# A vision tower layer on one core: tile loads three steps later in the sync engine's order, stores two steps later

## The chip, the cores and the metric

The kernel runs on one core of one Trainium2 chip. The metric is device time in microseconds (us) of one execution. Before the change three runs gave 1940.26, 1950.12 and 1956.40 us; their median is 1950.12 us.

## What is computed

The input x is 128 images of 12 channels by 224 by 224 in f32. The layer has three parts:

```python
pooled = x.reshape(Bb, Cc, n, K, n, K).sum(axis=(3, 5))          # 14 x 14 patches of 16 x 16
h = einsum('bcij,ce->bije', pooled, channel_weights)             # 196 tokens of 192 numbers
h = h + attn(layernorm(h))      # the first 64 tokens ask, the other 132 answer; projection of the result
h = h + ffn(layernorm(h))       # 8 routed experts of width 128, the best two of each token; one shared expert
```

The ffn computes `silu(x w1) * (x w3)` for each expert, multiplies it with the token's weight for this expert (zero for six of the eight), multiplies by `w2` and adds over the experts. The shared expert has no weight.

## The kernel before

**Groups, chunks, steps.** The images are worked in 8 groups of 16. The tokens of a group are split into 7 chunks: two of 512 query tokens, then key tokens in chunks of 512, 64, 512, 512 and 512. For each chunk all 9 experts are run one after the other, so a group has 63 steps (STEPS), step = 9 * chunk + expert. All engines follow this count. Every engine has its own program, in the same order of steps, and semaphores tie them together.

**One step.** TensorE (PE) makes h1 and h3 of this expert (L1275 for query chunks, with five products each, L1446 for key chunks), and between them the second layer of the step two before (L1426). ScalarE (ACT) takes silu of h1 (L803). GpSimd (POOL) multiplies it by the row of router weights of this expert, spread over 128 partitions (L654, in `scale`). VectorE (DVE) multiplies that by h3 (L1189) and counts `h_done`. PE may begin step s only when `h_done` of step s-2 is there. The shared expert (the ninth step of each chunk) needs no router weights.

**Router rows.** The weights of a group are computed one group ahead and written to a small array in HBM, `cw_rows`, in steps 57 to 59 (`cw_rows_out`, L496). `cw_load` (L520) reads one row of 512 weights back, spread over all partitions (256 KB written), into one of CW_RING = 7 buffers. The load for step s+5 (CW_AHEAD) stands at step s of the sync engine's order. It waits until the buffer is free, which is `h_done` of the use seven before.

**Tiles.** The images of a group come in 21 tiles of 1792 KB (`xt`, L461), into two slots. DVE sums five and four of a tile's 14 columns of patches in two parts (L841), ACT the other five (L699); 40 tiles at the start have another split, with POOL. The tiles for the group after the next are summed at the steps listed in LATE and EARLY: the first part in step s, the second in step s+1. The load of tile t+2 may be issued only when tile t has been summed, since it takes its slot. `load` therefore waits for `dve_summed` and `act_summed` of tile t. Before the change this load stands at step s of the sync engine's (SP) order, the step at which the engines begin to sum tile t.

**Stores.** `store` waits for the chunk's results to be copied out of PSUM (by DVE or ACT in the second step of the next chunk) and issues four DMAs of 96 KB (L481). Before the change it stands at the fourth step (e == 3) of the next chunk.

**The SP queue.** All loads and stores after the start are issued by SP, in the order in which `ffn_dma` writes them. SP carries them out one after the other: while one of them waits for its semaphore, none behind it is issued. Groups 0 to 5 (`left` = 2) sum tiles for later groups while their steps run. Group 6 (`left` = 1) does the attention work of group 7 (the items of PLAN) but sums no tile except the two of EARLY that belong to group 7. Group 7 has its 63 steps alone.

Of the kernel before, what the change touches and what calls it, by code (L numbers as in the profile page):

```python
# [35 lines left out]
NE, INTER = 8, 128  # L36
# [20 lines left out]
NCH = len(CHUNKS)  # L57
STEPS = NCH * EX
# [61 lines left out]
A_FIRST = 2  # L120
# [12 lines left out]
LINKS = 57  # L133


CW_RING = 7
CW_AHEAD = 5
CW_USES = NCH * NE
assert CW_USES % CW_RING == 0


LATE = {s: i for i, s in enumerate([4, 6, 8, 10, 12, 13, 16, 19, 22, 25, 29, 36, 38, 41, 46, 49, 52, 55, 58])}
EARLY = {0: 19, 1: 20}
POOL_TILES = TILES + len(LATE)

LATE0 = {s: i for i, s in enumerate([4, 6, 8, 10, 12, 14, 16, 18, 20, 22, 25, 28, 31, 34, 38, 44, 47, 50, 53])}

# [12 lines left out]
def pool_sums(g, t):  # L160

    return g.k is None and g.off * TILES + t < POOL_TILES


def tiles_at(g, step, groups_left=2):

    found = []
    if groups_left >= 1 and step in EARLY:
        found.append((g.plus(1), EARLY[step]))
    late = LATE0 if g.off < 0 else LATE  # L170
    if groups_left >= 2 and step in late:
        found.append((g.plus(2), late[step]))
    return found
# [53 lines left out]
def wait(eng, sem, value):  # L227

    if not isinstance(value, int) or value > 0:
        eng.wait_ge(sem, value)  # L230


def build(nc, x, cw, proj_w, proj_b, gate_w, gate_b, w1, w2, w3, sw1, sw2, sw3, out):
    ctx = ExitStack()
    with ctx:
        def sb(name, shape, dt=F32):
            return ctx.enter_context(nc.sbuf_tensor(name, shape, dt))

        def sem(name):
            return ctx.enter_context(nc.semaphore(name))  # L240
# [34 lines left out]
        HR = 3  # L275
        ffn = sb("ffn", [128, HR + 2 + CW_RING, 512])
        stage = sb("stage", [128, 2, 4, D])
# [20 lines left out]
        silu = [ffn[:, HR + i, :] for i in range(2)]  # L298
        cwb = [ffn[:, HR + 2 + i, :] for i in range(CW_RING)]
        cw_rows = nc.dram_tensor("cw_rows", (2, NE, CWCOL), F32).ap()  # L300
# [47 lines left out]
        cw_out = [sem("cw_out_first"), sem("cw_out_rest")]  # L348
        cw_landed = [sem(f"cw_landed{i}") for i in range(CW_RING)]
        l2_step, evac_dve, evac_act = sem("l2_step"), sem("evac_dve"), sem("evac_act")  # L350
# [32 lines left out]
        P_AT = {it: i for i, it in enumerate(PREP)}  # L383

        P_DVE = [kind in ("W0", "W1", "gate") or i % 2 == 0 for i, (kind, _) in enumerate(PREP)]
        P_DVE_N = [sum(P_DVE[:i + 1]) for i in range(len(PREP))]
        P_ACT_N = [i + 1 - P_DVE_N[i] for i in range(len(PREP))]
# [40 lines left out]
        def _(sp):  # L428
# [34 lines left out]
            def store(g, c):  # L463

                query, col, n = CHUNKS[c]
                st = stage[:, (g.par + c) % 2, :, :]
                done = out_stored[(g.par + c) % 2]
                if query:
                    sp.wait_ge(evac_dve, g.at(4, 2 * c + 2))
                else:  # L470
                    sp.wait_ge(evac_act, g.at(EVAC[-1], EVAC[c]))
                og = out.rearrange("(g b) t d -> g b t d", b=GB)[g.num()]
                for t in range((n + 127) // 128):
                    if query:
                        b0 = (col + 128 * t) // NQ
                        dst = og[b0:b0 + 2, 0:NQ, :]
                    elif n == 512:
                        dst = og[4 * t:4 * t + 4, NQ + col // GB:NQ + col // GB + 32, :]
                    else:
                        dst = og[:, TOK - 4:TOK, :]  # L480
                    sp.dma_start(dst, st[0:min(n, 128), t, :]).then_inc(done, 16)  # L481

            def load_after(g, t):

                if t + SLOTS < TILES:
                    load(g, t + SLOTS)
                elif g.k is not None or g.off < NG - 1:
                    load(g.plus(1), t + SLOTS - TILES)

            def cw_rows_out(g, step):  # L490

                for kind, i in items_at(step):
                    if kind == "C":
                        n = 512 if i < 6 else 64
                        sp.wait_ge(aux_act, g.at(BYACT[-1], BYACT[R[("C", i)]]))
                        sp.dma_start(cw_rows[g.par, :, 512 * i:512 * i + n], cw_stage[i][:, 0:n])\  # L496
                          .then_inc(cw_out[1 if i else 0], 16)

            def cw_load(g, step):

                c, e = divmod(step, EX)
                if e == NE:
                    return
                query, col, n = CHUNKS[c]
                use = c * NE + e
                slot = use % CW_RING
                def slot_free(use):

                    back = use - CW_RING
                    wait(sp, h_done, g.at(STEPS, back // NE * EX + back % NE + 1))  # L510

                if use == 0:
                    sp.wait_ge(cw_out[0], g.at(16, 16))
                elif use == NE:
                    sp.wait_ge(cw_out[1], g.at(96, 96))
                else:

                    slot_free(use + 1 if use + 1 in (NE, CW_USES) else use)
                at = col if query else 1024 + col
                sp.dma_start(cwb[slot][:, 0:n], cw_rows[g.par, e, at:at + n].partition_broadcast(128))\  # L520
                  .then_inc(cw_landed[slot], 16)

            def cw_ahead(g, step, left):

                if left:
                    cw_rows_out(g.plus(1), step)
                if step + CW_AHEAD < STEPS:
                    if g.off >= 0:
                        cw_load(g, step + CW_AHEAD)
                elif left:  # L530
                    cw_load(g.plus(1), step + CW_AHEAD - STEPS)

            def ffn_dma(g, left):
                for step in range(STEPS):
                    c, e = divmod(step, EX)
                    for gt_, t in tiles_at(g, step, left):
                        load_after(gt_, t)
                    cw_ahead(g, step, left)
                    if e == 3 and c > 0:
                        store(g, c - 1)  # L540
                store(g, NCH - 1)

            for t in range(TILES):
                load_after(G(None, 0), t)
            for step in range(A_FIRST, STEPS):
                for gt_, t in tiles_at(G(None, -1), step):
                    load_after(gt_, t)
                cw_ahead(G(None, -1), step, 1)
            ffn_dma(G(None, 0), 2)
            with sp.Fori(0, 2) as k:  # L550
                for off in (1, 2):
                    ffn_dma(G(k, off), 2)
            ffn_dma(G(None, 5), 2)
            ffn_dma(G(None, 6), 1)
            ffn_dma(G(None, 7), 0)
# [5 lines left out]
        def _(pool):  # L561
# [82 lines left out]
            def scale(g, step):  # L644
# [6 lines left out]
                slot = use % CW_RING  # L651
                pool.wait_ge(cw_landed[slot], g.at(16 * CW_USES // CW_RING, 16 * (use // CW_RING + 1)))
                pool.wait_ge(silu_done, g.at(STEPS, step + 1))
# [168 lines left out]
        def _(dve):  # L822
# [353 lines left out]
            def ffn_dve(g, left):  # L1176
                for step in range(STEPS):
# [7 lines left out]
                    else:  # L1185
                        dve.wait_ge(scaled, g.at(CW_USES, c * NE + e + 1))
                    dve.wait_ge(h3_ready, g.at(STEPS, step + 1))
# [18 lines left out]
        def _(pe):  # L1206
# [71 lines left out]
            def item(g, kind, i):  # L1278
# [27 lines left out]
                if kind == "tok":  # L1306
                    for s in (dve_summed, act_summed):
                        pe.wait_ge(s, g.at(TILES, TILES))
                    if pool_sums(g, 0):
                        pe.wait_ge(rows_used, min(POOL_TILES, g.at(TILES, TILES)))  # L1310
                    for k in range(CG):
# [173 lines left out]
```

## Time and profile before

| What | us |
|---|---|
| median of 3 runs (range) | 1950.12 (1940.26 to 1956.40) |
| the profiled execution | 1956.01 |
| its span, first to last instruction | 1954.3 |
| PE busy | 1616.2 (83%) |
| DVE busy | 1096.3 (56%) |
| ACT busy | 919.6 (47%) |
| POOL busy | 702.9 (36%) |
| mean granted TensorE clock | 0.909 of full |
| DMA, mean | 223 GB/s |

Groups are found in the trace by the 504 DVE products of L1189, 63 to a group: the last product of a group ends at 493.0, 715.6, 934.5, 1161.6, 1381.6, 1599.9, 1799.5 and 1944.6 us for groups 0 to 7. So group 1 runs from about 501 to 716 and group 6 from about 1607 to 1800. An idle time of an engine is written with what ended it. It counts only where the engine, or one that waits for it, is on the path to the end.

### The profile page before, as it was taken

To read this page: it belongs to the slowest core of one execution; us is meant where nothing else is said; L and a number is where in the kernel's file an instruction comes from. 1 tells how busy PE (TensorE), PEld (TensorE's weight loads), DVE (VectorE), ACT (ScalarE), POOL (GpSimd) and SP (SyncE) were. 2 spreads that over 40 slices of the span, in tenths; PEclk is the share of its full clock that TensorE was granted. 3 is DMA by queue.
4 is the path that set the end of the run, shared out by engine and by line. 5 is a ranking of instruction groups with operands and counts; after the bars stand their busy time and mean duration, and the time that the engine had idled before them with its cause. 6 is when DMAs were issued, how large, how long until landed. Compare 5 with 4: busy or idle time off the path is not lost.

```text
span 1954.3 us, 30301 instructions
## 1 busy us (share of the span) xinstructions
PE 1616.2 (83%) x9350; PEld 1262.1 (65%) x9350; DVE 1096.3 (56%) x1863; ACT 919.6 (47%) x3047; POOL 702.9 (36%) x687
## 2 busy tenths in 40 slices
PE   2715759987898789987898879987998879999988
PEld 1204538855786577855686667855786567867877
DVE  6845656557464766557456665567456663246233
ACT  2334446555474545644374545644474543433123
POOL 4335325223522334223332334323432334324344
PEclk9855669889998989989999899989999899989999
DMA  8887766667676676667666676657766672123233
GB/s 307 309 319 283 282 232 245 239 228 262 231 280 217 231 274 252 241 222 263 216 257 229 227 265 250 252 209 269 259 252 236 234 267 70 45 92 107 89 99 95
DMA packets 120850, 436.58 MB, mean 223 GB/s; under 512 B 20109, under 2 KB 49538, under 8 KB 99182
## 3 DMA queue, kind: packets, MB, share of 16 engines
q1 hardware_dynamic: 120470, 434.10, 61.6%
q8 instruction: 78, 1.28, 0.3%
q14 instruction: 86, 0.70, 0.1%
q10 hardware_dynamic: 216, 0.50, 0.1%
HBM read 413.86 MB, written 20.07 MB: 222 GB/s over the span
## 4 chain that ended last, share of the span: by engine, by line
PE 41%; DMA 17%; issue 13%; DVE 13%; POOL 7%; SPq 5%; ACT 2%; ACTq 0%; DVEq 0%; POOLq 0%
PE bank L1426 15%; DMA ffn<-cw_rows 13%; PE bank L1275 11%; POOL ffn L654 5%; DMA xt<-in_x 5%; DVE pooled L841 4%; PE bank L1446 3%; DVE ffn L1189 3%; POOL stat L629 2%; SPq L481 2%; PE bank L1372 2%; PE bank L1384 1%; SPq L461 1%; PE bank L1344 1%; PE bank L1333 1%
## 5 line engine op out<-in xcount | busy, mean ns | idle before, releaser
L654 POOL TENSOR_TENSOR ffn<-ffn 128x512 f32<-128x512 f32 (+1 forms) x448 | 512.8, 1149 | 1020.1 <-ACT ffn L803 653.2
L1426 PE MATMUL bank<-W2T,ffn 128*128 128x192 f32 (+1 forms) x3600 | 717.5, 339 | 0.0
L1189 DVE TENSOR_TENSOR ffn<-bank,ffn 128x512 f32<-128x512 f32 (+1 forms) x504 | 313.2, 622 | 696.9 <-POOL ffn L654 499.8
L1426 PEld LDWEIGHTS bank<-W2T,ffn 128*128 128x128 f32 (+1 forms) x3600 | 619.9, 195 | 50.5 <-issue 12.4
L803 ACT ACTIVATE ffn<-bank 128x512 f32<-128x512 f32 (+1 forms) x504 | 274.6, 547 | 441.9 <-PE bank L1446 278.6
L841 DVE TENSOR_REDUCE pooled<-xt 128x5 f32<-128x1280 f32 (+2 forms) x296 | 434.4, 1471 | 41.9 <-DMA xt<-in_x 40.9
L699 ACT ACTIVATE xt<-xt 128x256 f32<-128x256 f32 x800 | 322.9, 410 | 128.6 <-DMA xt<-in_x 128.3
L1446 PE MATMUL bank<-tokT,Wx 126*128 126x512 bf16 (+1 forms) x720 | 247.5, 365 | 97.6 <-DVE ffn L1189 97.1
L1446 PEld LDWEIGHTS bank<-tokT,Wx 126*128 126x128 bf16 x720 | 73.0, 102 | 180.6 <-DVE ffn L1189 134.1
L699 ACT ACTIVATION_READ_ACCUMULATOR xt<-xt 128x1 f32 x800 | 155.4, 194 | 0.0
L1275 PE MATMUL bank<-x0h,WT0h 128*128 128x512 f32 x288 | 142.3, 494 | 12.2 <-issue 5.7
L1275 PE MATMUL bank<-x1h,WT1s 128*128 128x512 f32 x288 | 114.8, 399 | 0.0
L1275 PE MATMUL bank<-x0h,WT0l 128*128 128x512 f32 x288 | 114.7, 398 | 0.0
L1275 PE MATMUL bank<-x1l,WT1s 128*128 128x512 f32 x288 | 114.6, 398 | 0.0
L1275 PE MATMUL bank<-x0l,WT0h 128*128 128x512 f32 x288 | 114.5, 397 | 0.0
L629 POOL TENSOR_TENSOR stat<-stat,mhalf 98x16 f32<-98x16 f32 x32 | 94.4, 2953 | 36.0 <-DVE stat L978 22.8
L614 POOL TENSOR_TENSOR kh_sum<-xt 128x256 f32<-128x256 f32 x40 | 29.4, 735 | 150.7 <-DMA xt<-in_x 150.7
L1372 PE MATMUL bank<-Msb,CWr 128*128 128x192 f32 x384 | 77.8, 343 | 0.0
L1275 PEld LDWEIGHTS bank<-x0h,WT0h 128*128 128x128 f32 x288 | 54.9, 190 | 26.6 <-DVE ffn L1189 11.0
L745 ACT ACT_TABLE_LOAD x28 | 35.9, 1283 | 65.5 <-DVE sums L1022 35.2
L768 ACT CAST tokT<-bank 126x256 bf16<-126x256 f32 x128 | 48.4, 381 | 37.9 <-PE bank L1365 37.9
L1372 PEld LDWEIGHTS bank<-Msb,CWr 128*128 128x128 f32 x384 | 64.4, 199 | 2.7 <-issue 0.3
(245 smaller groups left out, 1841.1 us busy)
## 6 DMA issues: line engine op xcount, KB each, us to landing
xt<-in_x SPq DMA_DIRECT2D x168, 1792.0 KB, 7.4
ffn<-cw_rows SPq DMA_DIRECT2D x384, 256.0 KB, 7.5
out<-stage SPq DMA_DIRECT2D x192, 96.0 KB
ffn<-cw_rows SPq DMA_DIRECT2D x64, 32.0 KB, 6.7
ffn<-in_L_ffn_w SPq DMA_DIRECT2D x2, 768.0 KB
attw<-in_L_ffn_w SPq DMA_DIRECT2D x1, 512.0 KB
Wx<-tokT ACTq DMA_DIRECT2D x9, 54.2 KB
out<-stage SPq DMA_DIRECT2D x8, 48.0 KB
```

Of the source, the lines that this page charges most:

```text
L481: sp.dma_start(dst, st[0:min(n, 128), t, :]).then_inc(done, 16)
L629: nc.gpsimd.tensor_tensor(out=stat[:, 3 * a + 1, u], in0=stat[:, 3 * a, u], in1=mhalf[0:HT, u], op=ALU.pow).then_inc(rstd_ready, 1)
L654: nc.gpsimd.tensor_tensor(out=cwb[slot][:, 0:n], in0=silu[(g.par + step) % 2][:, 0:n], in1=cwb[slot][:, 0:n], op=ALU.mult).then_inc(scaled, 1)
L699: last = nc.scalar.activation(src[:, :, j, :], src[:, :, j, :], ACT.Copy, accum_out=pooled[:, t // HALF, at:at + 1])
L768: nc.scalar.copy(dst[:, 0:2048].rearrange("p (c b k) -> p b c k", c=4, b=GB)[:, 2 * i:2 * i + 2, :, :], src[:, :, 0:128].rearrange("p b (c ...
L803: nc.scalar.activation(silu[p][:, 0:n], h_ps(g, step, 0)[:, 0:n], ACT.Silu).then_inc(silu_done, 1)
L841: ins = v.tensor_reduce(out=pooled[:, t // HALF, at + lo:at + hi], in_=src[:, lo:hi, :, :], axis=AX.XY, op=ALU.add)
L1189: v.tensor_tensor(out=h[step % HR][:, 0:n], in0=h_ps(g, step, 1)[:, 0:n], in1=(silu[p] if e == NE else cwb[(c * NE + e) % CW_RING])[:, 0:n ...
L1275: ins = mm(o, left[q], right[q], start=(q == 0), stop=(q == len(left) - 1))
L1372: last = mm(ps[:, 0:D], CWr[:, q, i % 4, :], Msb[:, i // 4, D * q:D * q + D], start=False, stop=(q == 2))
L1426: last = mm(o, h[step % HR][:, 128 * t:128 * t + m], W2T[:, e, :], start=(e == 0 and query and t % 2 == 0), stop=(e == NE), skip_group_che ...
L1446: last = mm(o[:, 0:n], Wx[:, w:w + INTER], X2T[g.par][:, col:col + n], start=True, stop=True)
```

## The change

```diff
+LOAD_BEHIND = 3
...
-assert CW_USES % CW_RING == 0
+assert CW_USES % CW_RING == 0 and max(LATE) + LOAD_BEHIND < STEPS
...
             def ffn_dma(g, left):
                 for step in range(STEPS):
                     c, e = divmod(step, EX)
-                    for gt_, t in tiles_at(g, step, left):
+                    for gt_, t in tiles_at(g, step - LOAD_BEHIND, left):
                         load_after(gt_, t)
                     cw_ahead(g, step, left)
-                    if e == 3 and c > 0:
+                    if e == 5 and c > 0:
                         store(g, c - 1)
                 store(g, NCH - 1)
...
             for step in range(A_FIRST, STEPS):
-                for gt_, t in tiles_at(G(None, -1), step):
+                for gt_, t in tiles_at(G(None, -1), step - LOAD_BEHIND) if step - LOAD_BEHIND >= A_FIRST else []:
                     load_after(gt_, t)
                 cw_ahead(G(None, -1), step, 1)
```

The lines of LATE, EARLY and POOL_TILES are moved and not changed. No instruction is added or taken away, on no engine. What is waited for by each load and each store stays the same, and so do the buffers. Only the place of the tile loads and of the stores among the loads of router rows changes, in the program of SP.

## Rows read from the trace of the kernel before

**Rows 1.** The page's first line: the span.
```profile
span 1954.3 us, 30301 instructions
```

**Rows 2.** The page's chain that ended last: shares of the span by line.
```profile
PE bank L1426 15%; DMA ffn<-cw_rows 13%; PE bank L1275 11%; POOL ffn L654 5%; DMA xt<-in_x 5%; DVE pooled L841 4%; PE bank L1446 3%; DVE ffn L1189 3%; POOL stat L629 2%; SPq L481 2%; PE bank L1372 2%; PE bank L1384 1%; SPq L461 1%; PE bank L1344 1%; PE bank L1333 1%
```

**Rows 3.** Waits of POOL, whole span: us in total, times, longest us.
```profile
POOL ffn L654 <- DMA ffn<-cw_rows: 366.5, 75, 9.5
```

**Rows 4.** Waits of SP's queue, whole span.
```profile
SPq L461 <- DVE pooled L841: 530.4, 148, 9.7
SPq L230 <- ACT xt L699: 470.6, 118, 12.0
SPq L520 <- DVE ffn L1189: 231.9, 131, 10.0
```

**Rows 5.** Timeline of SP, 656 to 682 us: start, us, engine, line, DMA, count.
```profile
656.21 0.34 SPq L461 DMA_DIRECT2D xt<-in_x  x1
656.66 2.63 SPq L520 DMA_DIRECT2D ffn<-cw_rows  x5
...
671.98 0.34 SPq L461 DMA_DIRECT2D xt<-in_x  x1
672.44 0.84 SPq L520 DMA_DIRECT2D ffn<-cw_rows  x2
...
679.65 1.44 SPq L461 DMA_DIRECT2D xt<-in_x  x1
```

**Rows 6.** Timeline of all engines, same stretch; in brackets the idle time before.
```profile
674.63 0.60 ACT L803 ACTIVATE ffn<-bank 128x512 f32<-128x512 f32 x1 [0.35 <-PE bank L1446]
...
678.28 1.21 DVE L841 TENSOR_REDUCE pooled<-xt 128x4 f32<-128x1024 f32 x1
...
680.53 2.48 POOL L654 TENSOR_TENSOR ffn<-ffn 128x512 f32<-128x512 f32 x2 [5.69 <-DMA ffn<-cw_rows]
...
681.98 0.69 DVE L1189 TENSOR_TENSOR ffn<-bank,ffn 128x512 f32<-128x512 f32 x1 [2.50 <-POOL ffn L654]
```

**Rows 7.** Tile cw_rows, 501 to 1600 us: issue to landing.
```profile
DMA to landing us min/median/max: 5.2/7.8/11.2
```

**Rows 8.** Tile cw_rows, 1607 to 1940 us: issue to landing.
```profile
DMA to landing us min/median/max: 2.8/3.3/7.2
```

**Rows 9.** Tile xt, 501 to 1600 us: issue to landing.
```profile
DMA to landing us min/median/max: 6.6/7.2/11.1
```

**Rows 10.** Windows, a group with tiles and group 6: busy us (instructions), clock, DMA, GB/s.
```profile
501.00:722.00 221.00, 195.65 (x1150) 155.20 (x1150) 131.30 (x225) 115.97 (x385) 77.09 (x62) 0.93 0.68 245
...
1607.00:1805.00 198.00, 189.30 (x1147) 150.88 (x1148) 89.09 (x186) 77.16 (x189) 76.70 (x61) 0.96 0.26 80
```

**Rows 11.** Line L1189, 501 to 722 us: who waited for it (us, times).
```profile
  PEld bank L1446: 19.7, 13
...
  PEld bank L1275: 3.1, 3
```

**Rows 12.** Line L1189, 1607 to 1805 us: who waited for it.
```profile
  PEld bank L1446: 7.8, 12
...
  PEld bank L1275: 1.9, 2
```

**Rows 13.** Windows of chunks 3 and 5, in group 1 and in group 6.
```profile
606.00:631.00 25.00, 18.34 (x109) 13.08 (x108) 13.18 (x44) 7.17 (x33) 4.07 (x9) 0.79 0.55 193
...
659.00:688.00 29.00, 20.45 (x100) 16.18 (x99) 21.42 (x40) 12.79 (x42) 10.05 (x8) 0.89 0.68 255
...
1710.50:1728.00 17.50, 16.29 (x117) 12.70 (x115) 9.88 (x40) 4.70 (x21) 4.16 (x9) 0.95 0.33 103
...
1759.00:1778.00 19.00, 17.35 (x97) 13.38 (x95) 17.58 (x34) 6.15 (x11) 10.48 (x9) 1.00 0.40 126
```

**Rows 14.** Waits of ACT and DVE for tiles, 501 to 1600 us.
```profile
ACT xt L699 <- DMA xt<-in_x: 13.0, 7, 3.5
...
DVE pooled L841 <- DMA xt<-in_x: 0.6, 1, 0.6
```

**Rows 15.** Timeline of ACT at 650 us: a wait for a tile.
```profile
650.02 0.42 ACT L699 ACTIVATE xt<-xt 128x256 f32<-128x256 f32 x1 [1.47 <-DMA xt<-in_x]
```

More of the change, by code:

```diff
@@ L133 @@
 LINKS = 57
+LATE = {s: i for i, s in enumerate([4, 6, 8, 10, 12, 13, 16, 19, 22, 25, 29, 36, 38, 41, 46, 49, 52, 55, 58])}
+EARLY = {0: 19, 1: 20}
+POOL_TILES = TILES + len(LATE)
+LOAD_BEHIND = 3
 CW_RING = 7
@@ L138 @@
 CW_USES = NCH * NE
-assert CW_USES % CW_RING == 0
-LATE = {s: i for i, s in enumerate([4, 6, 8, 10, 12, 13, 16, 19, 22, 25, 29, 36, 38, 41, 46, 49, 52, 55, 58])}
-EARLY = {0: 19, 1: 20}
-POOL_TILES = TILES + len(LATE)
+assert CW_USES % CW_RING == 0 and max(LATE) + LOAD_BEHIND < STEPS
 LATE0 = {s: i for i, s in enumerate([4, 6, 8, 10, 12, 14, 16, 18, 20, 22, 25, 28, 31, 34, 38, 44, 47, 50, 53])}
```

## The prediction, made before the changed kernel was run

> **What bounds the kernel now.** I read the chain that ended last first: under the matmuls, the largest single item on it is the landing of router rows, 13% of the span, some 250 us [rows 1, 2]. Next the waits of POOL: its multiply stood idle 366.5 us until such a row had landed, at 75 of 448 uses [rows 3]. Then the waits of SP's queue, to see why the rows come late: SP spends most of its time in front of tile loads, until DVE and ACT have summed the tile whose slot is wanted [rows 4]. The rows behind such a load are not late because the DMA engines are full; they have not been issued.
>
> One place shows the whole mechanism. SP issues a tile load at 656.21 and the next at 671.98 [rows 5]. Between them it issued five router rows and then sat in front of the tile load of step 46, which wants a sum that DVE makes in step 47. The two rows behind it go out at 672.44. The silu of step 51 is done at 674.63 + 0.60 = 675.23, but POOL starts its multiply at 680.53, when the row lands, 8 us after its issue [rows 5, 6]. POOL is 5.3 us late. DVE, which had its own sum until 679.49, waits 2.5 us more for POOL and makes h at 681.98 [rows 6].
>
> **What the change moves.** The moved instructions are, per group, 21 tile loads and 21 store DMAs (those of the first six chunks; the last chunk's store stays where it was). They pass loads of router rows in SP's queue, and no other queue is touched; POOL's, ACT's and DVE's orders are the same.
>
> *Router rows.* A row that stood behind the tile load of step s was issued at the gate of that load, the sum in step s+1. It was the row of step s+5 and had under four steps to land. Now the loads for steps s+5, s+6 and s+7 go in front of it; what holds them is only the free buffer, h_done of seven uses before, that is of about step s-2 to s. The first row behind the tile load is now that of step s+8. Even if SP sits at the gate until the sum of step s+1 is made, this row has more than six steps. A group of 63 steps takes 221 us [rows 10], 3.5 us a step; in chunk 3, the quickest, 25 us for nine steps, 2.8 us a step [rows 13]. Six steps are 17 us or more; the slowest landing among tiles is 11.2 us [rows 7]. So I expect nearly all row waits in groups 0 to 5 to go.
>
> *Tile loads.* They aren't later by three steps. SP reaches step s+3 when the row load of step s+2 has its buffer, at h_done of step s at the latest, and the sum in question is made on DVE behind h_done of step s+1. SP is still there before the gate opens, as it is now, and the load still goes out at the gate. Cost nothing; the cover is about one step (3 us). The tight place is the group's end: the load of LATE step 55 now stands at step 58, behind the rows written out at step 57. That may delay it by a step or so, for a tile needed only in the next group. The load of step 58 stands at step 61, behind the write-out of step 59, and its gate, the sum in step 59, opens in that same step.
>
> *Stores.* SP used to arrive at a store before the results were copied out. At e == 5 it arrives some two steps after. This wait goes from SP (the chain has SP's stores at 2% [rows 2]); I count nothing for it alone, since what stood behind it was router rows, already counted.
>
> **What it is worth.** The lateness of POOL isn't the gain, since DVE is often busy with a sum meanwhile (5.3 us became 2.5 above). PE carries the chain, so I price the gain where PE waits for h. In a group with tiles PE's weight loads stand idle for L1189 for 19.7 + 3.1 = 22.8 us [rows 11]. Group 6 has the same steps and the same attention work without late rows and tile sums: there it is 7.8 + 1.9 = 9.7 us [rows 12], and its row loads land in 3.3 us [rows 8]. The difference, 13.1 us per group, is what late rows and the DVE sums cost PE together; I take 12.5 for the rows. Six groups (0 to 5) have them: 75 us. The chunks agree: chunk 3 takes 25 us against 17.5 in group 6, chunk 5 29 against 19, but in chunk 5 DVE is busy 21.4 us of the 29, which no earlier row removes [rows 13]. Against this stands a cost: with shorter steps some tiles will be waited for, which is rare now (13.0 us at 7 places [rows 14]); at 650.02 ACT waited 1.47 us with no late row before it [rows 15]. I set 5 us for that. Sum: 75 - 5 = 70 us. The profiled execution took 1956.0 us, so 1886; the median of the runs is 6 us below it, so **1880 us**.
>
> *Bounds.* Upper: a group with tiles can't become quicker than group 6, 198 us against 221 [rows 10]: 23 us times 6 = 138 us, so 1956 - 138 - 6 = 1812. It would mean that DVE's extra 42 us of busy time and ACT's 39 cost nothing, which I don't believe, hence a value near half. Lower: the tile waits take most of it, about 15 us left, or the tiles are made worse (below).
>
> *The clock.* In chunk 3 the granted clock was 0.79 in group 1 and 0.95 in group 6 [rows 13]: full rate is 2.4 GHz, and the rest of the time is at 1.2. PE was idle for 6.7 of 25 us ahead of that. Fewer gaps should bring some back; it is inside the 23 us bound and I add nothing. The Trainium skill (TensorE: Matmul & The Clock Gate, Part 1) says that activity releases the throttle and idleness brings it back; the trace agrees in direction, and by it the result would lie below my sum and not above.
>
> **Rivals.**
>
> *Tiles take over, no measurable change.* Two slots mean that each load follows a sum and each sum follows a load. A landing takes 6.6 us at least [rows 9], about two steps. If steps get shorter, the next tile's landing becomes the wait of ACT and DVE, and h comes no earlier. For it: there is a wait for a tile already where no row was late [rows 15]. Against it: only 13.6 us of waits in five groups [rows 14], while row waits are far larger. If it eats four fifths of the 75 us, 15 us remain: 1935. Chance 0.12.
>
> *Slower: row loads and stores get in front of the tiles.* Before, SP had issued nothing for some time when a tile's gate opened, so a tile found empty DMA rings and the row loads went behind it. Now up to three row loads and a batch of stores may be in flight before it. A tile of 1792 KB lands in 6.6 us, so 256 KB ahead of it costs at most 6.6 x 256/1792 = 0.94 us, and a batch of four stores, 384 KB, 1.4 us. If half of the 126 tile loads of six groups had 1.4 us more, all of it on the path, that is 88 us; with half of the gain (35 us) kept it nets +53: 2003 us. It decides where the landing of a tile grows by more than the time that its sum can still wait, about 2 us. Against: rows are now issued one a step as buffers come free, at least one step before the gate, and a row alone lands in 3.3 us [rows 8], so most are through. Chance 0.05. The Trainium skill (DMA: Bandwidth & Descriptors, Queues, rings and completion order) says that each DMA engine takes descriptors in ring order. The trace agrees so far as rows behind a tile land in 7.8 us and rows without tiles in 3.3 [rows 7, 8]. By that rule alone this case would be the result.
>
> *Nearly all of the bound.* DVE and ACT sums slide into time that was idle; the clock recovers. Then 110 to 138 us: about 1830. Chance 0.12.
>
> *The change does not do what it says:* SP held by something else, the full ring of 7 buffers or the rows written out at steps 57 to 59, so that only part of the waits goes. Worth half, 35 us: 1915. It lies inside my own range.
>
> **How the numbers follow.** Forecast (1845 to 1925) 0.71, nearly all of the bound 0.12, no measurable change 0.12, slower 0.05. A measurement of this kernel tells about 1% from no change, 19.5 us. Faster by over 1% means under 1930.6 us: 0.71 + 0.12 = 0.83. Within 1%: 0.12. Slower: 0.05. The range for 8 in 10 takes in the forecast and the inner halves of its two neighbours: 1828 to 1933.
>
> **What the changed profile would show.** Right: POOL's wait for rows falls from 366.5 us to under 80; router rows leave the chain (13% to under 4%); groups 1 to 5 take about 209 us in place of 221; SP's row loads wait for h_done instead (L520 on L1189, 231.9 us before [rows 4], rises); tile loads still follow their gate at once and land in 7 to 8 us. Wrong: row waits gone but groups still at 218 us or more, with ACT's and DVE's waits for tiles up from 13.6 us to over 60 (tiles take over); or a median tile landing over 8.5 us (the slower case); or row waits that stay (SP held elsewhere).

## The result and the profile after

The changed kernel takes 1879.97 us (median of four runs, 1874.49 to 1882.55). The kernel before took 1949.11 us beside it. The ratio is 0.9643, 95% interval 0.9596 to 0.9691: 3.6% faster. The profiled execution took 1882.22 us.

The first line of the page and its chain, the rows that answer to [rows 1, 2] (line numbers are one higher than before):

```profile
span 1880.5 us, 30301 instructions
...
PE bank L1427 12%; POOL ffn L655 10%; PE bank L1276 7%; DMA xt<-in_x 7%; PE bank L1447 3%; DVE pooled L842 3%; POOL stat L630 3%; DVE ffn L1190 2%; PE bank L1373 2%; DMA ffn<-cw_rows 2%; SPq L482 1%; PE bank L1385 1%; ACT xt L700 1%; PE bank L1345 1%; PE bank L1405 1%
```

Router rows went from 13% of the chain to 2%, tile landings from 5% to 7%. The waits of POOL (us, times, longest) answer to [rows 3]:

```profile
POOL ffn L655 <- ACT ffn L804: 923.2, 380, 13.0
...
POOL ffn L655 <- DMA ffn<-cw_rows: 22.4, 4, 14.1
```

POOL now waits for ACT, as it should, and for rows only 22.4 us in place of 366.5. The waits of SP's queue, which answer to [rows 4]:

```profile
SPq L462 <- DVE pooled L842: 427.3, 128, 9.7
SPq L231 <- ACT xt L700: 362.1, 96, 12.0
SPq L521 <- DVE ffn L1190: 317.7, 171, 10.0
```

SP still waits a long time at tile gates. Its time in front of row loads, until a buffer is free, rose from 231.9 to 317.7 us. The same place as in [rows 5, 6], chunk 5 of group 1: SP's timeline, then POOL and DVE around step 51.

```profile
642.80 0.34 SPq L462 DMA_DIRECT2D xt<-in_x  x1
643.60 5.37 SPq L521 DMA_DIRECT2D ffn<-cw_rows  x4
656.53 0.34 SPq L462 DMA_DIRECT2D xt<-in_x  x1
656.98 0.84 SPq L521 DMA_DIRECT2D ffn<-cw_rows  x2
658.06 4.29 SPq L482 DMA_DIRECT2D out<-stage  x4
662.46 3.27 SPq L521 DMA_DIRECT2D ffn<-cw_rows  x1
```

```profile
661.42 0.68 DVE L1190 TENSOR_TENSOR ffn<-bank,ffn 128x512 f32<-128x512 f32 x1
...
663.26 1.27 POOL L655 TENSOR_TENSOR ffn<-ffn 128x512 f32<-128x512 f32 x1 [2.02 <-ACT ffn L804]
663.96 0.68 DVE L1190 TENSOR_TENSOR ffn<-bank,ffn 128x512 f32<-128x512 f32 x1
```

The products of steps 50 and 51 start 2.54 us apart, where they were 5.11 apart before (676.87 and 681.98); POOL is released by ACT. Who waited for h in group 1, and the windows of groups 1 and 6, answer to [rows 10, 11]:

```profile
  PEld bank L1447: 13.3, 14
...
  PEld bank L1276: 0.5, 1
```

```profile
487.00:696.00 209.00, 190.07 (x1153) 151.18 (x1152) 130.83 (x224) 117.14 (x391) 78.25 (x61) 0.96 0.71 259
...
1536.00:1731.00 195.00, 185.88 (x1153) 148.99 (x1151) 89.47 (x185) 79.58 (x201) 77.18 (x61) 0.98 0.28 90
```

Groups 1 to 5 took 221.4 us on average, measured from the last product of one group to the last of the next, and take 209.7 now. Group 0 went from 212.1 to 201.9 us, group 6 from 199.7 to 195.0, group 7 from 145.1 to 140.3; what comes before the first product got 4.4 us longer in this execution (284.6 us against 280.2; the same kernel has 280.1 in a later execution, e12, so this is no effect of the change). Together 5 x 11.7 + 10.2 + 4.7 + 4.8 - 4.4 = 73.8 us, as in the span. By chunk (mean of groups 1 to 5): chunk 3 went from 24.0 to 18.3 us, chunk 5 from 27.4 to 23.1, and no other moved by more than about 1 us. Their windows in group 1, which answer to [rows 13]:

```profile
599.00:618.00 19.00, 16.18 (x110) 11.82 (x108) 13.40 (x44) 6.54 (x31) 4.20 (x8) 0.89 0.61 222
646.00:669.50 23.50, 18.20 (x100) 13.84 (x100) 21.30 (x40) 12.22 (x42) 11.52 (x9) 1.00 0.68 236
```

Chunk 5 now is a DVE chunk: 21.3 us busy of 23.5.

### The profile page after: what moved, and what is told of

It is laid out like the page before. It is cut to its first block, busy times and chain, and to the rows that moved or that the text cites. A ratio compares the mean times of both kernels' runs of the same rounds, so it can differ in the third digit from the quotient of the medians.

```text
span 1880.5 us, 30301 instructions
## 1 busy us (share of the span) xinstructions
PE 1584.0 (84%) x9350; PEld 1242.6 (66%) x9350; DVE 1091.8 (58%) x1863; ACT 916.5 (49%) x3047; POOL 705.6 (38%) x687
## 4 chain that ended last, share of the span: by engine, by line
PE 31%; issue 30%; POOL 13%; DVE 11%; DMA 8%; ACT 3%; SPq 3%; ACTq 0%; POOLq 0%; DVEq 0%
PE bank L1427 12%; POOL ffn L655 10%; PE bank L1276 7%; DMA xt<-in_x 7%; PE bank L1447 3%; DVE pooled L842 3%; POOL stat L630 3%; DVE ffn L1190 2%; PE bank L1373 2%; DMA ffn<-cw_rows 2%; SPq L482 1%; PE bank L1385 1%; ACT xt L700 1%; PE bank L1345 1%; PE bank L1405 1%
## 5 line engine op out<-in xcount | busy, mean ns | idle before, releaser
L1427 PE MATMUL bank<-W2T,ffn 128*128 128x192 f32 (+1 forms) x3600 | 701.5, 334 | 0.0
L1427 PEld LDWEIGHTS bank<-W2T,ffn 128*128 128x128 f32 (+1 forms) x3600 | 608.7, 192 | 46.3 <-issue 4.8
L700 ACT ACTIVATE xt<-xt 128x256 f32<-128x256 f32 x800 | 323.3, 410 | 184.5 <-DMA xt<-in_x 184.3
L1447 PE MATMUL bank<-tokT,Wx 126*128 126x512 bf16 (+1 forms) x720 | 240.6, 355 | 53.1 <-DVE ffn L1190 52.1
L1405 PE MATMUL bank<-ident,gt 128*8 128x128 f32 x200 | 34.3, 323 | 54.0 <-DVE gt L1150 51.9
L1276 PEld LDWEIGHTS bank<-x0h,WT0h 128*128 128x128 f32 x288 | 54.8, 190 | 19.6 <-issue 7.3
L1405 PEld LDWEIGHTS bank<-ident,gt 128*8 128x8 f32 x200 | 18.5, 98 | 69.9 <-issue 55.8
```

The source lines that it names most:

```text
L700: last = nc.scalar.activation(src[:, :, j, :], src[:, :, j, :], ACT.Copy, accum_out=pooled[:, t // HALF, at:at + 1])
L1276: ins = mm(o, left[q], right[q], start=(q == 0), stop=(q == len(left) - 1))
L1405: last = nc.tensor.transpose(ps[0:NE, 128 * j:128 * j + 128], gt[:, 0, at:at + NE], ident[:, :])
L1427: last = mm(o, h[step % HR][:, 128 * t:128 * t + m], W2T[:, e, :], start=(e == 0 and query and t % 2 == 0), stop=(e == NE), skip_group_che ...
L1447: last = mm(o[:, 0:n], Wx[:, w:w + INTER], X2T[g.par][:, col:col + n], start=True, stop=True)
```

## The experiments

**1. Loads alone, stores alone, and the size of the step.** Four kernels ran side by side.

```diff
 e1: -                    if e == 5 and c > 0:      e2: -LOAD_BEHIND = 3
     +                    if e == 3 and c > 0:          +LOAD_BEHIND = 0
 e3: -LOAD_BEHIND = 3                               e4: -LOAD_BEHIND = 3
     +LOAD_BEHIND = 1                                   +LOAD_BEHIND = 4
```

Loads alone. 

> The changed kernel with the stores put back at the fourth step of a chunk; tile loads stay three steps later. Theory (the gain is the router rows, which no longer stand behind a tile's gate): POOL's wait for rows stays under 20 us, and nearly all of the gain is there, 1885 to 1895 us; the last two groups, which have no tile loads and got 4.7 us shorter each with the change, go back to their old length (199.6 and 145.1 us). Rival (the stores' wait and their four issues held up rows and tiles alike): 1920 us or more.

Measured: 1906.35 us, ratio 0.9777 (0.9728 to 0.9827). POOL's wait for rows is gone (4.4 us), and yet 26 us of the gain are missing, so the theory's price was wrong and the rival's too. Most of the missing time lies in one place: chunk 1 of groups 1 to 5 takes 51.3 us on average in place of 43.7 in the changed kernel (chunk 6 gives back 2.9 us of it). SP's timeline there, and what ACT and DVE wait for:

```profile
537.84 0.34 SPq L462 DMA_DIRECT2D xt<-in_x  x1
538.29 0.36 SPq L521 DMA_DIRECT2D ffn<-cw_rows  x1
538.95 8.73 SPq L482 DMA_DIRECT2D out<-stage  x4
548.01 1.72 SPq L462 DMA_DIRECT2D xt<-in_x  x1
```

```profile
558.37 0.41 ACT L700 ACTIVATE xt<-xt 128x256 f32<-128x256 f32 x1 [8.40 <-DMA xt<-in_x]
558.37 1.49 DVE L842 TENSOR_REDUCE pooled<-xt 128x5 f32<-128x1280 f32 x1 [5.51 <-DMA xt<-in_x]
```

SP needs 8.73 us just to issue the four stores, right behind a tile load. The tile load behind them is the one at step 13 of SP's order. It goes out 3.4 us after its gate has opened, lands 10 us later, and ACT stands 8.4 us, DVE 5.5. At e == 5 the same batch stands one step behind that tile load and hits the next tile, which can wait longer. Of the last two groups only group 7 went back to its old length (145.8 us); group 6 takes 194.5.

Stores alone. 

> The kernel before with the stores alone moved two steps later; tile loads stand at their old step. Theory: row waits of POOL stay at about 350 us, 1935 to 1945 us, what is gained lies mostly in the last two groups (about 10 us). Rival (stores): 1900 us or less, and POOL's wait for rows clearly down.

Measured: 1966.67 us, ratio 1.0102 (1.0055 to 1.0149). This is 1% slower; neither side had this, though POOL's wait for rows stayed as the theory said. The last two groups gained as expected (194.5 and 140.1 us), but that wait (351.9 us) moved: in chunk 2 the mean of groups 1 to 5 rose from 27.5 to 32.4 us. SP's timeline in group 1 and the POOL multiply behind it:

```profile
569.59 9.23 SPq L482 DMA_DIRECT2D out<-stage  x4
578.94 2.05 SPq L521 DMA_DIRECT2D ffn<-cw_rows  x1
581.31 0.34 SPq L462 DMA_DIRECT2D xt<-in_x  x1
```

```profile
587.15 1.26 POOL L655 TENSOR_TENSOR ffn<-ffn 128x512 f32<-128x512 f32 x1 [4.36 <-DMA ffn<-cw_rows]
```

The batch of stores now comes after SP has been held at a tile gate, and the row of step 20 is issued behind its 9.23 us. So the two parts of the change don't add: -42 us for the loads, +19 for the stores, but -69 together. With rows a step or more ahead a long batch makes none of them late (a tile load behind it can be, as in e1); with rows already late it makes them later.

One step. 

> The changed kernel with tile loads one step later than before in place of three. The first row behind a tile load is then that of step s+6, with over four steps to land. Theory (a row needs only to be issued some 9 to 11 us ahead, three to four steps): most of the row waits go, POOL's wait for rows under 100 us, 1890 to 1900 us. Rival (every step brings about a third of the gain): 1920 to 1930 us, wait for rows about 240 us.

Measured: 1884.68 us, ratio 0.9672 (0.9630 to 0.9714), 183.3 us of waits of POOL for rows in place of the under 100 expected. The time agrees with the theory and not with a third per step: one step brings all but about 5 us. The waits that are left hurt less: counted from the end of the silu to the start of POOL's multiply, rows are late by 14 us a group (mean of groups 1 to 5), against 32 before.

Four steps. 

> The changed kernel with tile loads four steps later. Theory (SP still arrives before the gate, since the gate opens behind h_done of step s+1 and the row load in front wants h_done of step s+1 at the latest): tiles go out at their gate or within 1 us of it, 1878 to 1886 us. Rival (no cover left, each tile load is pushed behind its gate): waits of ACT for tiles up by 30 us or more, 1895 us or more.

Measured: 1894.18 us, ratio 0.9720 (0.9676 to 0.9765). The price is nearly the rival's (1895 or more), the place another, and ACT's waits for tiles did not rise (186.7 us, against 184.3): most tile loads still go out at their gate, but those of tiles 19 and 20, moved to steps 59 and 62, stand behind the rows written out at steps 57 to 59 and leave 6.5 to 8.3 us behind their gate in groups 1 to 5. Chunk 0 of the next group takes 45.5 us in place of 42.2. In this kernel the group's end limits how far loads can be moved.

**2. A better place for the stores; the cause by another way; the price of a landing.** Four more kernels.

```diff
 e5: -                    if e == 5 and c > 0:      e6 (kernel before): -CW_AHEAD = 5
     +                    if e == 7 and c > 0:                          +CW_AHEAD = 6
 e8: LOAD_BEHIND = 2 and   if e == 6 and c > 0:
 e7: -                sp.dma_start(xt[:, slot, :], x_rows(g.num(), t)).then_inc(x_in[slot], 16)
     +                sp.dma_start(xt[:, slot, 0:ROW // 2], x_rows(g.num(), t)[:, 0:ROW // 2]).then_inc(x_in[slot], 16)
```

> The changed kernel with the stores four steps later than before (e == 7) in place of two; tile loads three later as in the change. A store batch then stands right behind a tile load in SP's order (steps 16, 25, 52, 61) and never right before one. Theory from the runs so far (a batch of four stores keeps SP busy for 4 to 10 us, and what it costs hangs on what stands behind it): the tile load that came 4 us behind its gate in chunk 1 comes at its gate, chunk 6 goes from 26.8 us back to about 24, 1862 to 1872 us. Rival (only SP's wait for the results counted, which is gone at e == 5 already): 1880 us.

Measured: 1857.22 us, ratio 0.9523 (0.9488 to 0.9559), better than both kernels, and 5 us below the theory's range. Its mechanism holds: next to no row is late, tile 6 (3 to 4 us behind its gate in the changed kernel) goes at its gate, chunk 6 takes 24.3 us in place of 26.8. A batch still keeps SP for 8.44 us, but now what stands behind it can wait:

```profile
554.48 0.34 SPq L462 DMA_DIRECT2D xt<-in_x  x1
554.98 0.32 SPq L521 DMA_DIRECT2D ffn<-cw_rows  x1
555.93 8.44 SPq L482 DMA_DIRECT2D out<-stage  x4
564.48 2.03 SPq L521 DMA_DIRECT2D ffn<-cw_rows  x1
```

> The kernel before with CW_AHEAD = 6 in place of 5: tile loads and stores stay where they were, and each router row is asked for one step earlier, so it passes one tile load and one store batch. Theory (late rows are the cause, and any way to issue them earlier brings the gain): POOL's wait for rows falls to a half or less (366 us before), 1890 to 1910 us. Rival (the gain comes from where tiles and stores stand to each other): 1935 us or more.

Measured: 1874.33 us, ratio 0.9606 (0.9564 to 0.9649), waits of POOL for rows 145.4 us. With tile loads and stores where they were, asking for each row one step earlier brings the whole gain of the change, 16 us more than the theory's better end. This separates the causes best: late rows are the cause, and the new places of tiles and stores are one way to cure it.

> The changed kernel, each tile load after the first two brings half of the tile's bytes only (the other half of the slot keeps old data), with all sums made as before. The start of the kernel gets shorter by this too, so read groups 1 to 5 (208.8, 207.6, 215.8, 208.0, 208.0 us in the changed kernel). Theory (ACT's waits for tiles, 59 us in five groups, and SP's long store batches are what keeps these groups above group 6, in part): 200 to 205 us per group. Rival (these waits lie beside other work; DVE's and ACT's sums are all of the difference): 207 us or more.

Measured: 1834.15 us; groups 1 to 5 take 202.8, 204.7, 211.6, 204.8 and 204.8 us, on average 205.7 against 209.7. Between the two expectations (200 to 205, 207 or more): shorter landings and shorter store batches are worth 4 us a group in the changed kernel. The kernel with stores at e == 7 gets nearly the same (206.1 us a group) with whole tiles, though ACT waits 32.1 us for tiles in its groups 1 to 5 and not at all here. This suggests that most of these waits cost little, but no run changes them alone. SP's batches of stores for chunks 0 and 1 of group 1:

```profile
511.29 6.95 SPq L482 DMA_DIRECT2D out<-stage  x4
...
547.53 5.28 SPq L482 DMA_DIRECT2D out<-stage  x4
```

In the changed kernel the same two batches take 10.03 and 7.82 us. With half the bytes in front of them SP gets through the stores sooner.

> The changed kernel with tile loads two steps later and stores three steps later (e == 6): again a store batch stands behind a tile load and not before one. Theory: row waits of a few us per group are left (one step later they were about 12 us of lateness per group, three steps later none), tiles as in the run with e == 7: 1865 to 1878 us. Rival (lateness of rows is all): 1880 to 1884, between the runs with one and with three steps.

Measured: 1860.39 us, ratio 0.9540 (0.9504 to 0.9575), 16 to 20 us better than the change (1879.97 us, 1876.36 when measured again). That speaks for the theory against the rival, though it is 5 us below the theory's range, and although rows still hold POOL for 61.5 us. It doesn't differ measurably from the kernel with three steps and e == 7. What the two share is that no batch of four stores stands right before a tile load.

**3. What is left, and what no longer matters.**

```diff
 e9  (on e5): +                if not pool_sums(g, t):
              +                    hi = lo + 1
                               ins = v.tensor_reduce(out=pooled[:, t // HALF, at + lo:at + hi], ...
 e10 (on e5): CW_AHEAD = 6
 e11 (kernel before): LOAD_BEHIND = 0 and   if e == 7 and c > 0:
```

> The kernel with tile loads three steps and stores four steps later (1857 us), in which DVE sums only one column of patches in each of its two parts of a tile, in place of five and four; the other columns are left unsummed, for all tiles that POOL has no part in. Everything else stays, tile loads and their gates too. Theory (what is left between a group with tiles, 204.5 us, and group 6, 194.5 us, is mostly DVE's sums standing in front of h): groups 1 to 5 fall to 195 to 199 us, 1815 to 1830 us. Rival (it is ACT's sums and tile landings): 202 us or more per group, 1845 us or more.

Measured: 1834.01 us; groups 1 to 5 take 204.1, 202.2, 205.8, 198.2 and 201.2 us, on average 202.3 against 206.1. The theory fell by this measure: leaving out most of DVE's sums takes away 3.8 us of the 11.6 us by which such a group is longer than group 6 (194.5 us); in all the kernel lies between the theory (1830 us or less) and the rival (1845 or more). The 3.8 us are a balance: chunk 5 falls from 23.1 to 19.6 us, close to group 6's 19.1, while chunk 6 gets 2.3 us longer. DVE's busy time is 94.28 us in this window of group 1, near group 6's 89.47:

```profile
489.00:685.00 196.00, 182.18 (x1113) 144.79 (x1112) 94.28 (x220) 111.25 (x371) 74.98 (x59) 0.96 0.74 271
```

What the other 8 us are, ACT's sums (111.25 us busy against 79.58 in group 6), landings or something else, stays open.

> The kernel with tile loads three and stores four steps later, and router rows asked for six steps ahead in place of five. No row is late there, so earlier rows can't help. Theory: same time, 1855 to 1865 us, or a little worse because tile loads then stand behind a row whose buffer comes free only at h_done one step later, next to the gate. Rival (some lateness of rows is still hidden in the time): under 1850 us.

Measured: 1860.35 us, ratio 0.9527 (0.9497 to 0.9557), the same as without it. Once no row is late, earlier rows bring nothing.

> The kernel before with the stores alone moved four steps later, tile loads at their old step. With two steps it was 1966 us, 1% worse than before. Theory (rows are late behind tile gates whatever the stores do, and a store batch of 4 to 10 us only moves which rows are late): POOL's wait for rows stays at 300 us or more, 1945 to 1975 us. Rival (the fourth step later is a better place for stores in itself): 1925 us or less.

Measured: 1979.93 us, ratio 1.0132 (1.0101 to 1.0164), 5 us above the theory's range. The place that is best for the stores once tile loads are moved (1857 us) is the worst while they are not. POOL's wait for rows is 388.5 us. The same mechanism as with two steps: SP is held at a tile gate until 585.42, then for 8.47 us in the batch, and two rows come very late:

```profile
585.42 0.34 SPq L462 DMA_DIRECT2D xt<-in_x  x1
586.23 0.32 SPq L521 DMA_DIRECT2D ffn<-cw_rows  x1
586.85 8.47 SPq L482 DMA_DIRECT2D out<-stage  x4
595.44 2.40 SPq L521 DMA_DIRECT2D ffn<-cw_rows  x2
598.15 0.34 SPq L462 DMA_DIRECT2D xt<-in_x  x1
```

```profile
602.28 1.26 POOL L655 TENSOR_TENSOR ffn<-ffn 128x512 f32<-128x512 f32 x1 [7.78 <-DMA ffn<-cw_rows]
```

The changed kernel once more beside these. 

> The changed kernel itself, beside the three others on the same chip: 1880 us, so that the kernel with stores at e == 7 (1857 us) and its relatives can be read against it directly.

Measured: 1876.36 us, ratio 0.9606 (0.9573 to 0.9639). Against 0.9523 (0.9488 to 0.9559) the kernel with stores at e == 7 is the better one; the intervals do not touch.

## Why the prediction was right, and where it was not

*The bound and the mechanism: right.* Rows stood behind tile gates. POOL's wait for them fell to 22.4 us (forecast: under 80), the chain's share to 2% (under 4%), groups 1 to 5 to 209.7 us (about 209). Run e6 shows the cause by another cut.

*The size of the row term: right as a sum, wrong in its parts.* The steps gave 75 us for six groups less 5 for tiles, 70. The six groups gave 5 x 11.7 + 10.2 = 68.7 us. But the estimator, PE's weight loads idle for h, fell from 22.8 to 13.8 us in group 1 and from 22.1 to 13.4 us on average in groups 1 to 5, so by 8.7 and not 12.5. The rest is the clock, which the prediction left at nothing. The last line of the windows of these five groups, before and after:

```profile
sum 1106.90, PE 970.80 PEld 768.33 DVE 660.38 ACT 586.22 POOL 387.33; mean PE 194.16 PEld 153.67 DVE 132.08 ACT 117.24 POOL 77.47
...
sum 1048.30, PE 948.09 PEld 753.82 DVE 655.89 ACT 583.97 POOL 389.83; mean PE 189.62 PEld 150.76 DVE 131.18 ACT 116.79 POOL 77.97
```

Of the 11.7 us a group, PE's idle time gave 7.2 us (27.2 to 20.0) and its busy time 4.5 us (194.16 to 189.62) for the same work, with the granted clock at 0.95 to 0.97 in place of 0.93 to 0.95. The row term was too large and the clock term too small by about the same amount. That they cancel is luck.

*Tile loads at no cost: wrong for two of 21.* On average they went from 0.2 to 0.8 us behind their gate. Tile 6 is 3 to 4 us late, for a reason that I hadn't named (the stores), and tile 20 about 4 us, at the group's end, which I had named, though for tile 19 (2 us).

*Tile waits, 5 us:* ACT and DVE waited 13.6 us for tiles in five groups [rows 14] and 65.8 us now. The rows after, for 488 to 1535 us:

```profile
ACT xt L700 <- DMA xt<-in_x: 61.3, 27, 4.1
DVE pooled L842 <- DMA xt<-in_x: 4.5, 5, 1.3
```

That is over the 60 us that was one half of my sign that tiles take over; the other half, groups still at 218 us or more, did not come, and they did not take over. Most of this wait lies beside other work: half tiles brought 4 us a group and took all of it away.

*"I count nothing for it alone" (the stores): wrong.* This is the step that failed. I saw only SP's wait for results and took the issue of four stores for free. Even that wait was misread: before the change SP waited for results at 17 of 56 stores, 52.0 us in all. Issuing them is SP's longest single job:

```profile
L482 SPq DMA_DIRECT2D out<-stage x129: 517/612/4452, 544.3 to 1592.4; - x129
```

One store takes 0.6 us to issue (median) and up to 4.45, and a batch for query tokens behind a tile load 7.2 to 10.1 us (8.5 to 10.8 before the change), against 4.4 in group 6 where no tile is in flight. The trace of before had it at 558.91, a batch of 8.66 us, and I read it as waiting. The stores' two steps are worth 26 us when loads are moved (e1 against the change) and cost 19 us when they are not (e2). That the forecast came out right without this term is in part luck. The same reasoning, applied to the loads alone, gave 1885 to 1895 us, and 1906 was measured. The changed kernel pays for its stores too, but less: with them at e == 7 (e5) it takes about 20 us less. The full cost shows in e1, e2 and e11.

*Groups 6 and 7: not foreseen.* They have no tile sums of later groups and still gained 9.5 us. One late row explains nearly all of group 7's 4.8 us. The silu and POOL's wait, then the window of chunk 4 before, and that of the changed kernel:

```profile
1889.72 0.60 ACT L803 ACTIVATE ffn<-bank 128x512 f32<-128x512 f32 x1 [0.59 <-PE bank L1446]
...
1892.78 2.48 POOL L654 TENSOR_TENSOR ffn<-ffn 128x512 f32<-128x512 f32 x2 [3.82 <-DMA ffn<-cw_rows]
```

```profile
1889.80:1911.10 21.30, 17.96 (x87) 14.14 (x87) 6.21 (x9) 6.02 (x11) 10.09 (x8) 0.84 0.59 174
```

```profile
1818.70:1835.40 16.70, 15.58 (x88) 11.35 (x87) 5.79 (x12) 5.92 (x13) 10.70 (x10) 1.00 0.65 209
```

POOL stood idle for 3.82 us. The silu was done at 1889.72 + 0.60 = 1890.32, so the row itself was 2.5 us late; then the granted clock of the stretch was 0.84 instead of full, and the chunk took 4.6 us more. This row goes with the place of the stores: group 7 takes 145.8 us in e1, with the stores at their old step, and 140.1 in e2.

Group 6's 4.7 us are nearly all the clock. PE is idle in it for 9.4 us before and 9.1 us after, but its busy time fell from 190.2 to 185.9 us. Most of this lies in chunk 4 (before, then after), where PE was never idle before the change:

```profile
1727.90:1758.70 30.80, 30.80 (x167) 20.91 (x166) 11.06 (x17) 13.32 (x26) 10.30 (x9) 0.80 0.28 88
```

```profile
1656.00:1684.00 28.00, 25.87 (x165) 16.49 (x164) 13.00 (x35) 10.79 (x34) 11.80 (x12) 0.94 0.35 115
```

Why the clock came back later in the one kernel is open. It goes neither with the loads nor with the stores: group 6 takes 194.5 us both in e1 and in e2, but 199.6 in e3, 203.0 in e4 and 202.4 in e6.

The Trainium skill (TensorE: Matmul & The Clock Gate, Part 1) says that idleness throttles and activity releases, and the trace agrees in group 7 and in groups 1 to 5, where less idle time went with a higher clock. Group 6 doesn't fit so simply: before the change the granted clock was 0.50 from 1730 to 1740 us, with PE busy in all of this stretch. The prediction said that by this rule the result would lie below its sum; in the six groups it made up what the other terms lacked.

*The rivals.* Slower by stores and rows in front of tiles: its mechanism exists and costs up to 7.6 us a group in e1. In the change's order it is much smaller, with tile 6 late by 3 to 4 us and a median tile landing of 7.6 us against 7.2, and the gain outweighs it. Tiles take over: no, as above.

## What to carry to other kernels

An in-order issuing engine is a resource of its own: a load with a late gate holds back everything behind it, so put it where its gate is just about to open and put in front of it what only needs to be early. Count the time in which each DMA is issued, not only its wait and its landing, and look at what stands right behind a long batch; moving the batch can turn from a loss of 19 us to a gain of 26 with the order around it. Two such moves don't add, so try them together.

## What the runs showed of the hardware

Issuing a store of 96 KB from SP took 0.6 us at the median and up to 4.45 us when a tile load of 1792 KB had gone out shortly before (up to 4.93 us before the change). Four of them took 2.3 us (key tokens) or 4.4 us (query tokens) with no tile in flight and 7.2 to 10.1 us (query tokens) behind one. Loads of router rows are held too: 0.37 us at the median and up to 3.27 us, right behind four stores. With half of each tile's bytes (e7) two of these batches took 6.95 and 5.28 us in place of 10.03 and 7.82, so what holds SP grows with what is in flight. That it is the queues behind SP, full of a tile's transfers, is argued from this; no run looks at the queues themselves.

A router row that came 2.5 us late made a chunk 4.6 us longer, with the clock down from full to 0.84 over it. Late data cost TensorE more than the lateness itself. In group 6 the same work took 4.4 us more of PE's busy time at a granted clock of 0.96 than at 0.98, with PE idle for equally long.
